# In every second unit of a state-space scan, the input product moves to ScalarE, TensorE and part of GpSimd, and the C product to GpSimd

## What is computed

```python
x_dbl = einsum('bkdl,kcd->bkcl', xs, x_proj_w)            # 8 dt rows, 16 B rows, 16 C rows
dts, Bs, Cs = split(x_dbl, [8, 24], axis=2)
dts = softplus(einsum('bkrl,kdr->bkdl', dts, dt_projs_w) + dt_projs_b)
A = -exp(A_logs)                                          # 4 paths x 256 channels x 16 states
def step(h, (u, dt, Bl, Cl)):
    h = h * exp(dt[..., None] * A) + (dt * u)[..., None] * Bl[:, :, None, :]
    return h, einsum('bkdn,bkn->bkd', h, Cl)
y = scan(step, 0) + Ds * xs
# paths summed, layer norm, times silu(z), output projection, plus x
```

## Time and profile before

| | before |
|---|---|
| median of three runs | 32,029.99 us |
| profiled execution | 32,048.26 us, span 32,046.2 |
| VectorE busy | 28,730.2 us, 90% of the span |
| GpSimd busy | 25,618.8 us, 80% |
| TensorE matmul busy | 23,441.0 us, 73% |
| ScalarE busy | 18,307.0 us, 57% |
| mean granted TensorE clock | 0.818 of full |
| DMA | 3,111 MB, 97 GB/s |

### The profile page before, as it was taken

How to read it: one execution, slowest core, us unless ns; L and a number is a source line. 1 busy time by engine, 2 the same in 40 slices (tenths; PEclk the granted TensorE clock), 3 DMA queues, 4 the chain that set the end, 5 groups by cost and what they waited for, 6 DMA issues and landing times. The chain is left out here.

```text
span 32046.2 us, 406694 instructions
## 1 busy us (share of the span) xinstructions
PE 23441.0 (73%) x112942; PEld 15851.8 (49%) x112942; DVE 28730.2 (90%) x27198; ACT 18307.0 (57%) x33418; POOL 25618.8 (80%) x11140
## 2 busy tenths in 40 slices
PE   5999976777777777777777777777777777777776
PEld 1555544444444444444444444444444444444444
DVE  7555548999999999999999999999999999999999
ACT  3444435565656656666665656666566666666565
POOL 4000008999999999999999999999999999999998
PEclk6999987887888887888888887887878887888877
DMA  3000023333333333333333333333333333333333
GB/s 133 26 26 26 26 104 98 105 104 104 106 107 104 104 105 104 104 104 104 105 106 105 104 104 106 105 105 104 104 105 104 104 104 105 107 105 104 104 106 95
DMA packets 1523713, 3111.30 MB, mean 97 GB/s; under 512 B 686811, under 2 KB 956667, under 8 KB 1252091
## 3 DMA queue, kind: packets, MB, share of 16 engines
q1 hardware_dynamic: 1518426, 3071.73, 31.3%
q10 hardware_dynamic: 4608, 33.82, 0.3%
HBM read 2935.45 MB, written 169.74 MB: 97 GB/s over the span
## 5 line engine op out<-in xcount | busy, mean ns | idle before, releaser
L1424 POOL TENSOR_TENSOR dbu<-dtu,bb 128x1024 f32<-128x1024 f32 x8192 | 19129.8, 2364 | 423.6 <-DVE hst L1359 385.1
L1359 DVE TENSOR_TENSOR_SCAN hst<-dA,dbu 128x1024 f32<-128x1024 f32 x8192 | 18516.5, 2275 | 232.8 <-ACT dA L1283 218.7
L1283 ACT ACTIVATE dA<-dtv,aneg 128x508 f32<-128x508 f32 x16384 | 10594.7, 678 | 6990.6 <-DVE hst L1359 6972.5
L1173 PE MATMUL yps<-ident,hc 128*128 128x128 f32 x65536 | 10744.2, 319 | 568.7 <-POOL hc L1434 560.7
L1173 PEld LDWEIGHTS yps<-ident,hc 128*128 128x128 f32 x65536 | 9592.0, 167 | 2495.5 <-issue 1146.4
L1367 DVE TENSOR_TENSOR hc<-hst,cps 128x1024 f32<-128x1024 f32 x6144 | 7341.2, 1195 | 708.0 <-PE cps L1148 674.9
L1148 PE MATMUL cps<-part,selc 96*128 96x512 bf16 x6144 | 2821.2, 459 | 5796.5 <-DVE hc L1367 5761.2
L1434 POOL TENSOR_TENSOR hc<-hst,cc 128x1024 f32<-128x1024 f32 x2048 | 4840.2, 2363 | 1366.0 <-DVE hst L1359 1365.7
L1148 PEld LDWEIGHTS cps<-part,selc 96*128 96x128 bf16 x6144 | 617.3, 100 | 8418.4 <-DVE hc L1367 8107.7
L1440 POOL TENSOR_TENSOR dtu<-dtv,xs 128x1024 f32<-128x1024 f32 x512 | 1209.1, 2361 | 4238.3 <-DVE dtv L1347 4238.3
L1086 PE MATMUL misc<-xg,wconv 128*128 128x512 f32 x4608 | 2436.9, 646 | 468.6 <-DMA xg<-xgp 467.8
(11 more groups left out here) (170 smaller groups left out, 21167.9 us busy)
## 6 DMA issues: line engine op xcount, KB each, us to landing
bb<-l_bscr SPq DMA_DIRECT2D x2048, 1024.0 KB, 10.7
cc<-l_bscr SPq DMA_DIRECT2D x512, 1024.0 KB, 9.9
xg<-xgp SPq DMA_DIRECT2D x512, 85.0 KB, 2.3
xgp<-xb ACTq DMA_DIRECT2D x32, 1032.0 KB, 9.7
xt<-in_x_dram SPq DMA_DIRECT2D x128, 256.0 KB, 2.8
l_xnT<-xo SPq DMA_DIRECT2D x128, 256.0 KB, 2.0
xn<-l_xnT SPq DMA_DIRECT2D x256, 128.0 KB, 2.1
xr<-in_x_dram SPq DMA_DIRECT2D x256, 128.0 KB, 2.2
```

The lines of the kernel that those rows point to most:

```text
L1173: mm = pe.matmul(yps[:, p, f * P:(f + 1) * P], hc[:, u % HB, f * 512 + p * P:f * 512 + (p + 1) * P], ident[:], is_transpose=True, start=fi ...
L1283: last = nc.scalar.activation(out[:, f, :, lo:hi], dtv[:, step % 2, f].rearrange("p (s l) -> p s l", l=P)[:, :, lo:hi], ACT.Exp, scale=ane ...
L1359: nc.vector.tensor_tensor_scan(hst[:, v % 4, way], dA[:, v % 2].rearrange("p f c -> p (f c)")[:, way], dbu[:, v % 4].rearrange("p f c -> p ...
L1424: nc.gpsimd.tensor_tensor(dbu[:, v % 4], dtu[:, step % 2], bb[:, v // 4 % 4, v % 4].unsqueeze(1).to_broadcast([P, 2, 512]), ALU.mult).then ...
```

## The change

Units alternate. **Even units** stay as they were (dbu by GpSimd, C spread by TensorE, C product by VectorE), with one PSUM `dA` buffer pair and two `dbu` buffers. **Odd ("turned") units**: B and dtu are transposed by TensorE once per path (`side`, 4 + 4 + 4 transposes through `cps`, copied by ScalarE to `bT` and `dtuT`), so that positions lie on the partitions and B is a scalar of each. `scale` multiplies four slices of 128 x 256 by that scalar, slices 0 and 1 on ScalarE, 2 and 3 on GpSimd; `fill` on TensorE turns them back with eight transposes into the PSUM bank pair `dbx`, which the scan reads, with its decay from SBUF (`dAs`). The C product of all odd units is GpSimd's. B and C are loaded as four states of the even or odd units at a time, two buffers each. `ln_shift` moves from VectorE to GpSimd (two small operations). The loops go in pairs of units, jobs have new places, the raw gate goes to a buffer of its own (`zraw`). PSUM stays full: 2 banks dA, 2 dbx, 2 yps, 1 cps, 1 misc.

```diff
-    ON_POOL = (2, 6, 10, 14)
+    HALF = UN // 2
+    ACT_P = (0, 1)
+    def turned(v):
+        return v % 2 == 1
+    POOL_P = tuple(p for p in range(4) if p not in ACT_P)
-        dA = ctx.enter_context(nc.psum_tensor("dA", [P, 2, 2, 512], F32))
+        dA = ctx.enter_context(nc.psum_tensor("dA", [P, 2, 512], F32))
+        dbx = ctx.enter_context(nc.psum_tensor("dbx", [P, 2, 512], F32))
...
-        XPROJ, DT0, DT1 = (0, 14, 35, 49), (5, 17, 38, 52), (7, 19, 40, 54)
-        OUT_AT = 21
-        DTU_AT = (11, 23, 44, 58)
+        XPROJ, DT0, DT1 = (0, 16, 32, 49), (4, 20, 36, 52), (6, 22, 38, 54)
+        OUT_AT = 41
+        DTU_AT = (9, 25, 41, 57)
...
-        for q, u in enumerate((3, 4)):
+        for q, u in enumerate((3, 10)):
             JOBS[u] = ("post", "unpermute", q)
-        for q, u in enumerate((10, 11)):
+        for q, u in enumerate((19, 35)):
             JOBS[u] = ("post", "turn_back", q)
-        for f, u in enumerate((22, 23)):
+        for f, u in enumerate((8, 9)):
             JOBS[u] = ("own", "gate", f)
-        TAPS = ((0, 2, 4, 6, 8, 9), (0, 1, 3, 5, 7, 8, 9))
-        for f, u in enumerate((24, 29)):
+        TAPS = ((0, 2, 4, 6, 8, 9), (0, 2, 3, 4, 5, 6, 7, 8, 9))
+        for f, u in enumerate((11, 24)):
...
+            for k, at in enumerate((4, 10, 12)):
+                SIDE[16 * q + at] = (kind, (q + 1) % 4, k)
-        DS_AT, LN_AT, GATED_AT, SILU_AT = (7, 8, 9, 10), 6, 13, 37
+        DS_AT, LN_AT, GATED_AT, SILU_AT = (7, 8, 9, 10), 12, 39, 40
...
@@ SyncE @@
+                def load_c(q, b):
+                    step = q // 2
+                    if not (isinstance(b, int) and 8 * b + q < 2):
+                        sp.wait_ge(s_hcp, b * HALF + (4 * q - 4))
+                    sp.dma_start(cc[:, q % 2], bscr[step % 2, 8 * (q % 2) + 1:8 * (q % 2) + 8:2].partition_broadcast(P)).then_inc(s_cld[q % 2], 16)
...
                     write_b(ph, 1, b)
+                    load_b(2, b)
+                    load_c(2, b)
                     if "pre" in ph.kinds:
                         sp.wait_ge(s_mf, ph.misc(("own", "gate", 1)))
                         load_xg(b + 1)
+                    load_b(3, b)
+                    load_c(3, b)
+                    write_b(ph, 2, b)
...
@@ TensorE @@
+                def fill(v, b):
+                    if ACT_P:
+                        pe.wait_ge(s_dba, b * HALF + (v // 2 + 1))
+                    if POOL_P:
+                        pe.wait_ge(s_dbp, b * HALF + (v // 2 + 1))
+                    wait(pe, s_scan, b * UN + (v - 1))
+                    for p in range(4):
+                        for f in range(2):
+                            mm = pe.transpose(dbx[:, f, p * P:(p + 1) * P], dbT[:, v // 2 % 2, p, f * P:(f + 1) * P], ident[:])
+                    mm.then_inc(s_fill, 1)
...
+                    for u in range(0, UN, 2):
+                        if u + 3 < UN:
+                            fill(u + 3, b)
+                        elif not last:
+                            fill(u + 3 - UN, b + 1)
+                        if u:
+                            total(u - 1, b)
+                        elif not (isinstance(b, int) and b == 0):
+                            total(UN - 1, b - 1)
+                        pe.wait_ge(s_hc, b * HALF + (u // 2 + 1))
+                        c = SIDE.get(u)
+                        if ph.has(c):
+                            side(c[1], c[2], at(ph, c[0]))
+                        job_of(ph, u)
+                        total(u, b)
+                        if ph.has(c):
+                            pe.wait_ge(s_ce, (at(ph, c[0]) * 4 + c[1]) * 3 + (c[2] + 1))
+                        if u + 2 < UN:
+                            spread_c(ph, u + 2)
...
+                        job_of(ph, u + 1)
...
@@ ScalarE @@
+                def scale(v, b):
+                    step, st = v // NST, v % NST
+                    if st == 1:
+                        act.wait_ge(s_ce, (b * 4 + step) * 3 + (3 if max(ACT_P) > 1 else 2))
+                    wait(act, s_fill, b * HALF + (v // 2 - 1))
+                    for p in ACT_P:
+                        last = nc.scalar.mul(dbT[:, v // 2 % 2, p], dtuT[:, step % 2, p], bT[:, step % 2, p, st:st + 1])
+                    last.then_inc(s_dba, 1)
...
+                    for u in range(0, UN, 2):
                         if u + 2 < UN:
                             decay(ph, u + 2, b)
+                        take_of(ph, u - 1)
+                        if u + 3 < UN:
+                            decay(ph, u + 3, b)
+                        c = SIDE.get(u)
+                        if ph.has(c):
+                            side(c[1], c[2], b + 1 if c[0] == "pre" else b)
...
                         if u == SILU_AT:
+                            silus(ph, not last, True, b)
+                        if u + 5 < UN:
+                            scale(u + 5, b)
+                        take_of(ph, u)
...
@@ VectorE @@
+                    if turned(v):
+                        dve.wait_ge(s_fill, b * HALF + (v // 2 + 1))
+                        wait(dve, s_hcp, b * HALF + (v // 2 - 1))
+                        decays, inputs = dAs[:, v // 2 % 2], dbx
+                    else:
+                        dve.wait_ge(s_inp, b * HALF + (v // 2 + 1))
+                        wait(dve, s_hc, b * HALF + (v // 2 - 1))
+                        decays, inputs = dA, dbu[:, v // 2 % 2]
...
-                        if not on_pool(u):
+                        if not turned(u):
                             times_c(u, b)
...
@@ GpSimd @@
+                def scale(v, b):
+                    step, st = v // NST, v % NST
+                    if st == 1:
+                        pool.wait_ge(s_ce, (b * 4 + step) * 3 + 3)
+                        nc.gpsimd.tensor_tensor(heldp[:], zeros[:, 0:1], zeros[:, 1:2], ALU.add)
+                    for p in POOL_P:
+                        last = nc.gpsimd.tensor_scalar(dbT[:, v // 2 % 2, p], dtuT[:, step % 2, p], bT[:, step % 2, p, st:st + 1], None, ALU.mult)
+                    last.then_inc(s_dbp, 1)
...
+                    for u in range(0, UN, 2):
+                        if u + 4 < UN:
+                            inputs(u + 4, b)
+                        times_c(u + 1, b)
+                        if u + 5 < UN:
+                            scale(u + 5, b)

```

More of the change, by code:

```diff
@@ L886, in layer1 @@
         s_hcp = sem("s_hcp")
-        s_cld = sem("s_cld")
+        s_cld = [sem(f"s_cld{q}") for q in range(2)]
+        s_fill = sem("s_fill")
+        s_dba = sem("s_dba")
+        s_dbp = sem("s_dbp")
+        s_cf = sem("s_cf")
+        s_ce = sem("s_ce")
         s_cb = sem("s_cb")
@@ L892, in layer1 @@
         s_bst = sem("s_bst")
-        s_bld = [sem(f"s_bld{q}") for q in range(4)]
+        s_bld = [sem(f"s_bld{q}") for q in range(2)]
         s_soft = sem("s_soft")
@@ L1031, in _ @@
                 write_b(PRO, 0, 0)
-                for q in range(4):
+                for q in range(2):
                     load_b(q, 0)
+                    load_c(q, 0)
                 def body(ph):
@@ L1148, in spread_c, with side @@
                     pe.matmul(cps[:, :], selc[:, u % NST], part[:, u // NST % 2], start=True, stop=True).then_inc(s_cb, 1)
+                def side(step, k, b):
+                    n = b * 4 + step
+                    if k == 0:
+                        for p in range(4):
+                            mm = pe.transpose(cps[:, p * P:(p + 1) * P], xdbl[:, step % 2, p * P:(p + 1) * P], ident[:])
+                    else:
+                        if k == 1:
+                            pe.wait_ge(s_dtu, n + 1)
+                        for p in range(2):
+                            for f in range(2):
+                                at = (2 * (k - 1) + p) * P
+                                mm = pe.transpose(cps[:, (2 * p + f) * P:(2 * p + f + 1) * P], dtu[:, step % 2, f, at:at + P], ident[:])
+                    mm.then_inc(s_cf, 1)
@@ new lines, in total @@
+                def total(u, b):
+                    if turned(u):
+                        pe.wait_ge(s_hcp, b * HALF + (u // 2 + 1))
+                    else:
+                        pe.wait_ge(s_hc, b * HALF + (u // 2 + 1))
+                    first = u % 32 == 0
+                    for p in range(4):
+                        if first and p % 2 == 0 and (u or not (isinstance(b, int) and b == 0)):
+                            pe.wait_ge(s_yout, b * 4 + (2 if u else 0) - 1 + p // 2)
+                        for f in range(2):
+                            mm = pe.matmul(yps[:, p, f * P:(f + 1) * P], hc[:, u % HB, f * 512 + p * P:f * 512 + (p + 1) * P],
+                                           ident[:], is_transpose=True, start=first and p % 2 == 0 and f == 0,
+                                           stop=(u % 32 == 31), skip_group_check=True)
+                    mm.then_inc(s_y, 1)
+                    if u in DS_AT:
+                        p = DS_AT.index(u)
```

(32 more changed lines are left out.)

208 lines of the change are left out of this document (96 added, 112 removed).

## The result

The changed kernel takes 33,109.79 us (median of four runs, 33,104.82 to 33,121.27) against 32,026.37 beside it; the ratio is 1.0339 (95% interval 1.0321 to 1.0357). I had forecast 29,775, in a range of 29,200 to 31,300.

A forecast was written before the change was run, and what follows sets the result against it. VectorE set the pace before, GpSimd close behind. After: VectorE 183.1 plus 8.0 waits is 191.1, GpSimd 191.3, plus 3 for overlap, 194 a block; 194 x 128 + 4,961.6 = 29,794 profiled, 29,775 us median; range 29,200 to 31,300.

The forecast's parts named there:

- the bound on GpSimd's scaling: GpSimd, 64 new 128x256 scalings: step between 0.15 and 0.69 us, taken as 0.48, 30.7 us a block.
- The slower rival: GpSimd's 64 scalings cost 0.79 us or more each, making the kernel slower than before; chance 0.06.
- 3 us for imperfect overlap: Added per block because VectorE and GpSimd, nearly equal at 191.1 and 191.3, don't overlap perfectly; gives 194.
- a rule of the Trainium skill: GpSimd one-input operations run roughly at line rate: scaling 0.21 us above the fixed part, leading to the cheap case (0.14).
- VectorE's sum: VectorE per block: 64 scans at 2.20, 32 C products at 1.11, softplus 5.4, statistics 1.4; 183.1 us, 19.2 less.
- the 8.0 that I carried over: VectorE's waits of 8.0 us a block before the change, added unchanged to 183.1 to give 191.1.
- GpSimd's other terms: GpSimd per block besides scalings: 69 products at 2.31, 159.4 us, and six tiny operations, 1.2 us.
- the rival of TensorE's order: TensorE's single queue, at clock 0.80, makes the block some 10 us longer, 204, or 31,060 us; chance 0.09.
- TensorE and its clock: TensorE load 147 us a block at the high clock, 184 at mean 0.80; granted clock expected above 0.80.
- The wait for xg: First conv job on TensorE, waiting 3.65 us behind the gate job; most of that was to go.
- ScalarE was forecast at 168 busy a block: ScalarE: 127.7 busy today, plus 64 scalings at 0.52 (33), 12 copies (7), 0.7 zero columns; 87% of the forecast.
- the prediction's signs of being wrong: Scaling outside 0.35 to 0.65, a scan's price changing with its operands' places, or ScalarE's side copies holding TensorE.

The follow-up runs named there:

- e10: Changed kernel with each of GpSimd's two 128x256 scalings replaced by a product of two full tensors (input product half wrong); 31,448 us.
- e2: Changed kernel with GpSimd's two scalings by an immediate 0.5 instead of a pointer (input product half wrong); 32,444 us.
- e11: Changed kernel with GpSimd's two scalings made one of 512 columns by an immediate 0.5 (input product wrong); 31,709 us.
- e9: Kernel before with the new job order alone (job places, separate gate buffer, SyncE's order), units as before; 31,163.81 us, ratio 0.9734.
- e12: e3 with odd units alternating between two and three slices on ScalarE, the rest one broadcast product on GpSimd; 30,078.02 us, ratio 0.9394.
- e8: e3 with six of the eight transposes of fill left out, so only the first slice is turned back; 29,782 us.
- e3: Changed kernel with GpSimd's two scalings made one 512-column product with B broadcast, nothing left out; 30,560.99 us, ratio 0.9546.
- e4: Changed kernel with three slices scaled on ScalarE and one on GpSimd, nothing left out; 30,400.36 us, ratio 0.9507.
- e6: e4 with GpSimd's fourth slice as a 256-column product with B broadcast instead of a scaling; 30,717.73 us, ratio 0.9599.
- e5: Changed kernel with GpSimd's scalings left out (its slices zeroed once, waits for them removed); 30,273 us.

## Why the prediction was wrong

**The step that failed** is the bound on GpSimd's scaling: "two inputs at 256 columns would be 0.74, a step of about 0.69 ... That is the upper end, as the scaling reads one tensor." Measured, the step of two tensors is 0.69 (e10), and that of the scaling 0.895. I took an order of prices for granted (one stream cheaper than two) that no row showed, and called its consequence a bound. The term was 64 x 0.48 = 30.7 and is 57.3, 26.6 us a block or 3,400 us, and the forecast was off by 3,335. The slower rival had the mechanism, its place and the point from which it decides: its sum has a step of 0.75 (the 0.79 in its text doesn't follow from that sum), and 0.895 lies beyond it. It had 6% because the false bound spoke against it. By its formula 160.6 + 3 + 57.3 = 220.9, 33,220 us, within 0.4% of what came, in part by luck: its 3 us for imperfect overlap weren't there, and the products and tiny operations were 2.1 more.

The prediction also weighed a rule of the Trainium skill (GPSIMD Engine Reference, section 4.1), one-input operations at roughly line rate. It pointed the same false way. For this form the trace disagrees: 2.50 ns a column with an immediate (e2, e11), against 2.13 between full-tensor products of 256 and 1024 columns (e10, 0.686 and 2.325 us). The measurement decides.

**VectorE's sum** was right: scans unchanged, C products 1208 ns, nmr gone. What the forecast left out is that the new job order takes VectorE's waits from 8.0 us a block to 1.4 in the old kernel (e9). I read the waits and did not ask which of them the moved jobs would end; 176.4 of the 264.7 us were waits for C's spread, and 1.2 are left. In the alternating kernel others come in their place, 11.8 us a block in e12 and 9.9 in e8, so the 8.0 that I carried over came near by chance.

**GpSimd's other terms**: 69 products x 2.31 = 159.4 were 32 x 4.66 + 11.6 = 160.7, the tiny operations 2.0 instead of 1.2. Near enough.

**The 3 us for imperfect overlap** were not there in the changed kernel, as GpSimd waited for almost nothing. For a kernel as cheap as the forecast they were too few. e12 has 187.5 of GpSimd's own work, less than I had forecast, and takes 196.5; e3 194.4 and takes 200.2. With a scaling at 0.48, the block would have been an estimated 198 rather than 194, between these two. Part of that is shown to be TensorE's (e8, 5.7 us in e3); part in e4 and e12 is the wait for dA (187 to 258 us in 7000), that is ScalarE's order of decays, scalings and job copies. So the rival of TensorE's order was half right: it has a price, of about 6 us, but it isn't what decided.

**TensorE and its clock.** Forecast above 0.80; it is 0.92, and 0.92 to 0.94 in the complete versions with GpSimd relieved. The forecast gave fill as the reason, which keeps the engine busy in stretches where it stood idle; e9 shows that the job order alone, with no more matmuls, takes it to 0.87, so fill can have given at most the rest. The rule cited there from the Trainium skill (TensorE: Matmul & The Clock Gate, Part 1), that activity releases the throttle, agrees with the rise from 0.80 to 0.92. By e9 the amount of work isn't all of it: the same matmuls got 0.87. The wait for xg is gone: no idle time before the conv matmuls, where it was 3.65 us. **ScalarE** was forecast at 168 busy a block and is 157, its scaling 0.45 instead of 0.52. An activation of dAs (to SBUF) has 710 ns on the row, one of dA (to PSUM) 676, but two of them take 1.33 and 1.30 us together, so both have a step of 0.62:

```profile
20032.72 1.30 ACT L1367 ACTIVATE dA<-dtv,aneg 128x508 f32<-128x508 f32 x2
...
20034.78 1.33 ACT L1367 ACTIVATE dAs<-dtv,aneg 128x508 f32<-128x508 f32 x2
```

**DMA** hid as forecast: no engine waits for bb or cc. Of the prediction's signs of being wrong one came, the scaling outside 0.35 to 0.65; the scans kept their price, and ScalarE's side copies kept C's spread on TensorE waiting for 0.7 us in the whole run.

**What the change is made of**, then, in us a block: the job order -6.7 (e9 against before). Alternating the units, as written, +15.2 (220.1 against 204.9). The same with one broadcast product in place of two scalings: -4.7 (e3); with the load spread over both engines by e12: -8.4.

**TensorE's stop** once a block is a wait for its instructions. The pages list among the DMA queues (packets, MB, share), first the kernel before, then the changed kernel and e8:

```profile
q8 instruction: 23, 0.38, 0.0%
...
q8 instruction: 1406, 23.04, 0.3%
...
q8 instruction: 1151, 18.86, 0.3%
```

e3 has 1,406 too, and e8 differs from it by six TensorE transposes in every odd unit, so this queue brings TensorE's instructions. The trace has the start of each packet. In e6 every one of the 125 stops of over 1.5 us (from 5,000 us on, in the yps matmuls) ends 2.15 to 2.52 us after a packet of q8 starts, with a median of 2.32; in e5 the 125 stops end 2.15 to 2.53 us after one, with a median of 2.33. Some eleven packets come in a block, and only the one at the loop's jump is followed by such a stop; that the jump is what makes it late is argued from its place.

The packet comes at this place in the other kernels too (125 of 127 blocks in the changed kernel, e3, e4, e6 and e12), and in none of these does the fourth of the eight matmuls start less than 2.15 us after it. What differs is how long the fill ahead of them waits. On average that is 3.58 us in the changed kernel (for GpSimd's scaling), and for a scan 3.54 in e3, 3.01 in e4, 2.50 in e12 and 1.78 in e6. The longer that wait, the less of the stop is left to be seen. **Open** is what ends it. A loop body with fewer TensorE instructions wasn't tried; the kernel before has 23 packets in all.

## What to carry to other kernels

A bound needs a row or a reason on each side: "cheaper than that, since it reads less" was neither, and one look at that form alone (a run like e2 or e10) would have told faster from slower. When work is moved to an engine that is 93% busy, the sum of that engine's start-to-start steps is the forecast: where the step was known beforehand to a few hundredths of a us, the time came within 0.5% (e10 31,400 and 31,448, e11 31,850 and 31,709). Where an engine multiplies by a scalar per partition, compare the scaling with a product whose second operand is broadcast, in one longer instruction.
